# A two-layer macaron block on one core: the first layer norm with tokens as rows, zero fills on three engines, expert weights loaded in another order

## What is computed

```python
x = L0_attn_x                                                   # (2, 1024, 128)
x = x + 0.5 * _L0_ffn_ref(_layernorm(x, axis=-1), L0_ffn_Wg, L0_ffn_W_in, L0_ffn_W_out)
x = x + _L0_attn_ref(_layernorm(x, axis=-1), ...)
...
# _layernorm: (x - mean) / sqrt(var + 1e-5), over the 128 features
# _L0_ffn_ref: logits = xf @ Wg; softmax; top 2 of 8 experts; a token is
# dropped where its place in the expert is past C; gates normalised;
# hid = inp @ W_in; a, g = split(hid); out = (gelu(a) * g) @ W_out; y = sum of gates * out
```

## Time and profile before

| | us |
|---|---|
| median of 3 runs (lowest, highest) | 1421.39 (1421.01, 1423.98) |
| profiled execution, own time | 1424.82 |
| its span | 1423.0 |
| PE busy | 1323.8 (93%) |
| VectorE busy | 1005.4 (71%) |
| ScalarE busy | 871.2 (61%) |
| GpSimd busy | 400.2 (28%) |
| mean granted PE clock | 0.981 |

### The profile page before, as it was taken

The page is one execution under the profiler, slowest core; times in us unless marked ns, Lnnn a source line. Parts: engine busy times, 40 slices in busy tenths (PEclk is TensorE's granted clock), DMA queues, the critical chain, the costliest instruction groups (busy, mean ns, idle before and its releaser), DMA issues.

```text
span 1423.0 us, 27091 instructions
## 1 busy us (share of the span) xinstructions
PE 1323.8 (93%) x10934; PEld 562.0 (39%) x10934; DVE 1005.4 (71%) x1516; ACT 871.2 (61%) x1104; POOL 400.2 (28%) x331
## 2 busy tenths in 40 slices
PE   7999998889879999999999998989998999999997
PEld 5344333333324444333444343433433334433443
DVE  3534777889925347698887868688868697978735
ACT  3334347788784454276566767666768676675672
POOL 5554430110011755452220223022305033202010
PEclk8999999999999999999999999999999999999998
DMA  6633101000001731011111010110010101100100
GB/s 177 118 62 70 25 14 31 16 2 2 2 1 39 196 60 34 1 32 24 35 24 24 1 23 1 24 35 10 15 24 1 23 13 24 31 13 19 24 1 15
DMA packets 30291, 45.80 MB, mean 32 GB/s; under 512 B 5892, under 2 KB 10692, under 8 KB 30116
## 3 DMA queue, kind: packets, MB, share of 16 engines
q1 hardware_dynamic: 30168, 44.08, 14.0%
HBM read 25.39 MB, written 1.18 MB: 19 GB/s over the span
## 4 chain that ended last, share of the span: by engine, by line
PE 72%; DVE 11%; ACT 8%; issue 4%; SPq 3%; DMA 2%; POOL 0%; ACTq 0%; DVEq 0%
PE ps L1264 13%; PE ps L1364 11%; PE ps L1309 7%; ACT PR L1442 6%; PE ps L1230 5%; PE ps L1250 5%; PE ps L1231 5%; PE ps L1232 5%; DVE BM L1530 3%; PE ps L1844 3%; PE ps L1328 2%; PE ps L1242 2%; PE ps L1271 2%; PE ps L1375 2%; PE ps L1324 1%
## 5 line engine op out<-in xcount | busy, mean ns | idle before, releaser
L1442 ACT ACTIVATE PR<-ps 128x1024 f32<-128x1024 f32 x432 | 431.2, 1026 | 207.1 <-PE ps L1271 136.4
L1530 DVE TENSOR_REDUCE BM<-ps 128x2 f32<-128x1024 f32 (+2 forms) x384 | 350.4, 950 | 57.0 <-PE ps L1250 55.9
L1264 PE MATMUL ps<-QS,KS 48*128 48x512 f16 (+7 forms) x2688 | 306.1, 329 | 31.7 <-ACT PR L1442 22.5
L1364 PE MATMUL ps<-PR,VS 128*32 128x512 f32 (+3 forms) x2304 | 231.5, 499 | 2.2 <-ACT PR L1442 1.6
L1264 PEld LDWEIGHTS ps<-QS,KS 48*128 48x128 f16 (+1 forms) x2688 | 108.5, 95 | 203.6 <-ACT PR L1442 88.5
L1250 PE MATMUL ps<-KS,QS 48*128 48x128 f16 (+2 forms) x1728 | 161.7, 273 | 19.2 <-DVE BM L1530 10.8
L1523 DVE TENSOR_REDUCE BM<-ps 128x8 f32<-128x1024 f32 x96 | 116.8, 1220 | 39.3 <-PE ps L1250 38.5
L1250 PEld LDWEIGHTS ps<-KS,QS 48*128 48x128 f16 x1728 | 68.0, 94 | 135.3 <-issue 45.8
L1571 POOL TENSOR_TENSOR OS<-OS,RX 128x512 f32<-128x512 f32 x24 | 30.5, 1270 | 273.9 <-ACT RX L1458 273.9
L1230 PE MATMUL ps<-YA,QS 128*128 128x512 f16 x256 | 99.6, 389 | 0.8 <-DVE RX L1489 0.5
L1231 PE MATMUL ps<-YA,QS 128*128 128x512 f16 x256 | 99.2, 388 | 0.0
(11 more groups left out here) (299 smaller groups left out, 2054.9 us busy)
## 6 DMA issues: line engine op xcount, KB each, us to landing
PR<-gates SPq DMA_DIRECT2D x32, 512.0 KB, 12.5
QS<-KS SPq DMA_DIRECT2D x64, 128.0 KB
QS<-KS SPq DMA_DIRECT2D x64, 64.0 KB
WM<-W_in SPq DMA_DIRECT2D x1, 2048.0 KB, 9.0
QS<-HL SPq DMA_DIRECT2D x48, 32.0 KB
KS<-HL SPq DMA_DIRECT2D x48, 32.0 KB
QS<-CT SPq DMA_DIRECT2D x96, 2.0 KB
KS<-KS SPq DMA_DIRECT2D x8, 128.0 KB, 2.4
```

Source lines behind the costliest of these rows:

```text
L1264: ins = pe.matmul(ps[pair][:, w, off:off + cols], KS[rows, ks, kt * P:(kt + 1) * P], QS[rows, qs, (ph + 1) * TT - cols:(ph + 1) * TT], sta ...
L1364: ins = pe.matmul(dst[32 * j:32 * j + 32, TT - cols:TT], v, PR[:, buf, j, off:off + cols], start=(g == 0), stop=(g == NGRP[ph] - 1))
L1442: act.activation(dst, src, ACT.Exp, scale=0.125 if lat else 1.0).then_inc(sig["exp"], 1)
L1530: ins = dve.tensor_reduce(BM[:, ph, p, :, qt - 4 * ph, part], bnk[:, :, off:off + nk * P], AX.X, ALU.max)
```

## The change

- x comes in four DMAs, one a tile, each with its own semaphore. It stands with a token as a row (`XR`, 16 blocks of 128 tokens).
- VectorE takes mean and variance of each row: per tile four `bn_stats` and four `bn_aggr`, on 128 x 128 each. ScalarE takes ln and exp of 128 x 4 values, VectorE makes the shift (L997), and ScalarE scales and shifts four 128 x 128 blocks a tile into `XS`. PE turns `XS` by 16 more transposes, VectorE copies them to `XN`. The matmuls with the mean matrix and the 512-wide square, ln, exp, subtract and multiply of this norm are gone. x itself is still turned and copied to `XT`.
- `KS` is cleared by VectorE (6 pieces, first of all) and GpSimd (10), `QS` by ScalarE (8, before its first-part tasks).
- `W_in` is issued right behind the folded weights and `Wg0`, then `W_out`, then the rest. Waits are for `W_in` alone where the experts start, for the others at `ed` 0.
- 12 of the 16 heads of `pe_comp` stand between the transposes of tiles 1 to 3. The last four, and `pe_comp_out`, are plan tasks (`cmp` 0 and 1). `eh` u waits for them from u = 4, since the ring's places lie over their inputs.
- The constants of `sp_first_consts` are issued behind the eighth `egb`.

The diff, cut to its core:

```diff
+        if kind in ("rlg", "rrk", "rtp", "cmp"):
             return 0
...
+            x = add("DVE", "eh", ("eh", u), x, ("ed", u - self.NHE) if u >= self.NHE else self.staged(u))
...
+            self.add("ACT", "cm", ("cmc", i), self.add("PE", "cm", ("cmp", i), ("rlg",)))
...
-            sp.dma_start(PRf[:, 0:T].rearrange("p (i d) -> p i d", i=NTT),
-                         a["x"].rearrange("(i p) d -> p i d", p=P)).then_inc(s_x0, 16)
+            for t in range(NT):
+                sp.dma_start(XR[:, t, :, :], a["x"].rearrange("(t i p) d -> t p i d", p=P, t=NT)[t]).then_inc(s_x[t], 16)
...
+            sp.dma_start(w_in, a["W_in"].rearrange("e p f -> p e f")).then_inc(s_wm, 16)
...
         def pe_load(pe):
+            pe.wait_ge(s_const, 1)
             for t in range(NT):
+                pe.wait_ge(s_x[t], 16)
+                for i in range(4):
+                    ins = pe.transpose(bank(t)[:, i * P:(i + 1) * P], XR[:, t, i, :], identf[:, :])
+                ins.then_inc(s_ld, 1)
             for t in range(NT):
+                pe.wait_ge(s_xc, t + 1)
+                if t >= 2:
+                    pe.wait_ge(s_xn, t - 1)
+                for i in range(4):
+                    ins = pe.transpose(bank(5 + t % 2)[:, i * P:(i + 1) * P], XS[:, t, i, :], identf[:, :])
+                ins.then_inc(s_ld, 1)
+                if t == 1:
+                    pe.wait_ge(s_wc, 80)
+                if t >= 1:
+                    pe_comp(pe, range(4 * t - 4, 4 * t))
...
+            for h in range(ZDVE):
+                dve.memset(KS[:, h, :].bitcast(F32), 0.0).then_inc(s_zero, 1)
+            stats(0)
             for t in range(NT):
+                if t + 1 < NT:
+                    stats(t + 1)
+                shift(t)
+                if t >= 1:
+                    normal(t - 1)
+                if t < NT - 1:
+                    plain(t)
+            normal(NT - 1)
+            plain(NT - 1)
...
+                for i in range(4):
+                    ins = act.activation(XS[:, t, i, :], XR[:, t, i, :], ACT.Identity, scale=RSTD[:, t, i:i + 1],
+                                         bias=SHIFT[:, t, i:i + 1])
+                ins.then_inc(s_xc, 1)
+            act.wait_ge(s_const, N_CONST)
+            for h in range(8):
+                act.activation(QS[:, h, :].bitcast(F32).rearrange("p (a c) -> p a c", a=2),
+                               goon[:, :].unsqueeze(1).to_broadcast([P, 2, 256]), ACT.Copy, scale=0.0).then_inc(s_zero, 1)
```

More of the change, by code:

```diff
@@ L321, in weights_ready, with staged @@
     def weights_ready(self, u):
+        return None
+    def staged(self, u):
         return None
@@ L428, in weights_ready, with staged @@
         return ("ewl", min(u // 2, E - 1))
+    def staged(self, u):
+        return ("cmp", 1) if u >= 4 else None
     def prologue(self, b):
@@ L675, in priority @@
         if eng == "PE":
-            if kind in ("un", "sc", "pv", "turn", "proj", "eu", "ed", "rlg", "rrk", "rtp"):
+            if kind in ("un", "sc", "pv", "turn", "proj", "eu", "ed", "rlg", "rrk", "rtp", "cmp"):
                 return super().priority(eng, task, t)
@@ L826, in build_program @@
         gate_d = nc.dram_tensor("gates", (4, E, T), F32, kind="Internal").ap()
-        s_x0 = sem("s_x0")
+        s_x = [sem(f"s_x{t}") for t in range(NT)]
         s_w = sem("s_w")
@@ L946, in pool_const, with pe_comp @@
                 ins = pool.memset(desc[:, e:e + 1], float(E - e))
-            pool.memset(epsc[:, 0:1], EPS)
             ins = pool.memset(epsc[:, 1:2], EPS * EPS)
             ins.then_inc(s_const, 1)
+        def pe_comp(pe, heads):
+            for h in heads:
+                ins = pe.matmul(bank(4)[:, h * 32:(h + 1) * 32], wqn[:, h, :], wkb[:, h, :], start=True, stop=True)
+            return ins
         def pe_load(pe):
             pe.wait_ge(s_const, 1)
-            pe.wait_ge(s_x0, 16)
@@ L1488, in dve_attn @@
                     dve.wait_ge(sig["ed"], c("ed", u - plan.NHE))
+                elif not lat and u >= 4:
+                    dve.wait_ge(sig["cmp"], 2)
                 dve.scalar_tensor_tensor(out=ring_he(lat, u), in0=ps[plan.slot[("eu", u)]][:, 1, :],
@@ L1613, in pe_first @@
                     ins.then_inc(sig["val"], 1)
-                else:
+                elif kind == "cmp":
+                    i, = args
+                    if i == 0:
+                        ins = pe_comp(pe, range(H - 4, H))
+                    for h in range(H if i else 0):
+                        g, j = divmod(h, QUAD)
+                        ins = pe.matmul(bank(5)[32 * j:32 * j + 32, g * P:(g + 1) * P], wkb[:, h, :],
+                                        won[h // 8][:, h % 8, :], start=True, stop=True)
+                    ins.then_inc(sig["cmp"], 1)
+                else:
+                    if task == ("eu", 0):
+                        pe.wait_ge(s_xup, NT)
+                    elif task == ("ed", 0):
+                        pe.wait_ge(s_w, N_WFIRST)
                     pe_attn(pe, False, c, plan, task)
@@ L1619, in act_first @@
             table = First.table
-            act.wait_ge(s_wm, 32)
             for task in plan.order["ACT"]:
                 kind, args = task[0], task[1:]
+                if task == ("ewh", 0):
+                    act.wait_ge(s_wm, 16)
                 want = First.TABLE.get(kind, table)
@@ L2361, in _ @@
             sp_load(sp)
-            sp_first_consts(sp)
             sp_first(sp)
```

115 lines of the change are left out of this document (46 added, 69 removed).

## The result

| | before | after |
|---|---|---|
| median of 20 runs (lowest, highest), us | 1424.03 (1420.33, 1431.77) | 1416.82 (1411.55, 1424.27) |
| span of the profiled execution | 1423.0 | 1417.0 |
| router logits end | 32.68 | 28.17 |
| gates leave for DRAM | 43.82 | 40.69 |
| first down projection (`ed` 0) starts | 54.41 | 49.92 |

The ratio after / before is 0.9949 (95%: 0.9933 to 0.9964). Against 1421.4 us that is a gain of 7.2 us (5.1 to 9.5), where 4.4 were forecast: 1414.2 on the scale on which the forecast was 1417.0. The time came out inside the range and on the forecast's side, 2.8 us past it.

The account below looks back on a forecast made before the run. It took the preface's chain of waits through PE, then a full PE from 60 to 150 us, as the bound. Gates leaving at 39.4 instead of 43.8 gain 4.4 us: 1421.4 - 4.4 = 1417.0 us, range 1411 to 1420.

Parts of the forecast that it names:

- Up to the logits: Part from the start to the end of the router logits, forecast to end at 26.1 us instead of 32.7.
- T: The time the router logits end; forecast 26.1 us instead of 32.7.
- Scaling: ScalarE's four 128-wide scaling operations per tile of the norm, put at 1.0 us.
- VectorE has 1.4 us to spare: In the norm, PE's folding was to end last at 19.4 us, with VectorE having 1.4 us of slack.
- Between the logits and the gates: Folding holds rrk, three eu hold rtp; 2.2 of 6.6 us given back, gates stored at 39.4, gain 4.4.
- stays at 1.2 GHz all through: PE's preface, with nothing wide in it and transposes not counted as busy work, was to run at half clock throughout.
- the clock's return: PE's return to full clock in eu 1 to 3: -2.1 us if full at once, +1.8 if all half.
- the early one as a rival: Full clock only from eu 0: gates leave at 36.5, gain 7.3 us; within the full-clock-earlier rival, chance 0.20.
- Absorbed behind 150 us: Rival: behind 150 us VectorE and ScalarE share the bound, half the gain could go; 1419 to 1420 us, chance 0.15.
- reshuffled neighbours: Unknown from tasks changing places in the plan, put at +-1 us on the total.
- Hidden edits: ScalarE's and GpSimd's fills, earlier weights and later constants were to be covered by other work; earlier load alone gives nothing.
- the rival of a full clock from the start: PE at 2.4 GHz from the first folding: gates leave at 30 to 33.4, gain 10.4 and more; full-clock-earlier chance 0.20.

Follow-up runs that it names:

- norm_order: Changed kernel with scaled tile 0 turned before x's tile 3 and tile 3's statistics taken before the first XN copy; 1417.01 us, 0.9965 of the kernel before.
- fills_pool: Changed kernel with all 24 zero fills on GpSimd, none on VectorE or ScalarE; 1420.51 us, 0.9983 of the kernel before.
- wide_between: Changed kernel with extra unread 512-column matmuls on zeros added to PE's preface and logits; 1410.43 us, 0.9902 of the kernel before.
- plan_alone: Kernel before with only the plan's change: the last four heads and pe_comp_out become tasks behind eu 0; 1422.13 us, 0.9985 of the kernel before.
- before_again: Kernel before, unedited, profiled once more; 1422.12 us, one run.
- gates_first: Changed kernel with VectorE's copy of the turned gates moved directly behind router step 21; 1419.47 us, 0.9971 of the kernel before.
- fold_ahead: Changed kernel with all folding ahead of the logits again and the old plan, new norm and fills kept; 1423.07 us, 1.0003 of the kernel before.
- after_again: Changed kernel, unedited, timed and profiled once more; 1418.22 us, 0.9964 of the kernel before.
- weights_late: Changed kernel with W_in and W_out issued last again; 1418.69 us, 0.9954 of the kernel before.

## Why the prediction was right

**Up to the logits: right in shape, 2.1 us short.** T was forecast at 26.1 and came at 28.17. Fills (0.53 each, 3.19 in all, for 3.8 forecast), statistics (1.2 a tile, for 1.4) and shift (0.13) were no dearer than taken. Two terms were too small. *Scaling:* four ScalarE activations of 128 columns took 1.65 us, not 1.0. I had scaled 0.55 for 512 columns down; 0.41 for 128 says that most of it doesn't go with width. *x:* the last quarter landed at 9.09 (7.4 to 9.1 in the traces where it is on the chain), not 7.7; with the logits 19.1 us behind it, that alone is 1.4 of the 2.1 us. With PE in order, the turn of the scaled tile 0 stood behind it, and so did VectorE, with the statistics of tile 3 and the shift of tile 2 queued. norm_order took that coupling out and had the folding done at 19.37. That the forecast said 19.4 is luck in part, since it priced the scaling 0.65 us a tile too low. I had written "VectorE has 1.4 us to spare"; it had none. The logits took 6.92, for 6.7.

**Between the logits and the gates: right in mechanism.** The folding held `rrk` until 34.38, 6.2 us behind the logits (6.0 forecast). `rtp` had no idle time before it and stood behind `eu` 3, 11.5 us behind the logits (12.2 forecast). 1.4 us of the 4.5 were given back (2.2 of 6.6 forecast). The two errors cancel in part: the gates left at 40.69, where 39.4 was forecast, so 3.1 us sooner than before instead of 4.4, and in the executions where the clock returned early at 37.0 to 38.0. `et` 0 started 7.8 us behind the store (7.9 forecast), PE stood 0.66 us for it (1.1 forecast), and `ed` 0 came 4.5 us earlier though the gates were only 3.1 earlier, because PE wasn't held for `rtp` and its clock didn't fall again. `ed` 4 now stood ahead of `eu` 12, as forecast, and both were done at about 57.6 instead of 61.46, 3.9 earlier (4.4 forecast).

**The clock: right for after ahead of the logits, too narrow behind them.** The preface ran at half clock all through in after, and in five more of the seven profiled executions that have the new norm and nothing added on PE. The seventh is fills_pool: PE had run transposes and nothing else, and its next four took 0.66 us and the folding behind them 1.07, before the clock fell again ahead of the turn at 13.60. "TensorE: Matmul & The Clock Gate", Part 4: PE-mode transpose, of the Trainium skill, says that transposes don't count as busy work for the clock. After agrees with it (0.22 to 0.28 us a transpose, 0.11 to 0.17 in wide_between), fills_pool doesn't, so the prediction's "stays at 1.2 GHz all through" holds in most executions, not in all. It cost nothing there, since PE stood 1.29 us for ScalarE right behind. The folding passes of 32 columns and the logits of 8 ran at half clock from 16.5 to 28.2 us in after. What I had wrong is that I took the clock's return as one value with a tolerance (-2.1 to +1.8). It is two cases, 30 and 37 us, in the same kernel, 2.9 us of lead apart (0.75 of them x), and I had booked the early one as a rival instead of as part of the forecast.

**From 60 to 200 us: right.** The lead of 4.1 holds. **Absorbed behind 150 us: wrong way round.** I put reshuffled neighbours at +-1 us, and gave 0.15 to half of the gain being lost. They gave 3.3 us net by 441 in the trace of after, and 2.2 in plan_alone. That is the term of the sum that was mis-sized most, and with it fails the sign that every landmark between 100 and 400 us would be earlier by the same amount. It is of the size of the 2.8 us between 1417.0 and 1414.2, though these are themselves within what a second timing of the same kernel moved. I had seen the swaps in the plan, but judged them by the amount of work ahead of each task, which says nothing on who waits for whom: 19 waits for ScalarE instead of 17 can't be read from it.

**Hidden edits: right.** Earlier weights gave nothing. ScalarE's fills ran from 17.63 to 21.88 and GpSimd's from 16.10 to 20.78, beside folding and logits that lasted to 28.17, as forecast.

**The sums.** Three don't come out as written. Gates that leave at 30 to 33.4 give a gain of 10.4 to 13.8, so 1407.6 to 1411.0 for the rival of a full clock from the start, not 1410.4. The clock's return "if full at once" was put at -2.1 us, but VectorE asks for the turned gates only at 36.8, so by the prediction's own rows it is worth 1.5. And the listed unknowns add up to 1413.4 to 1420.7, wider than the 1414.5 to 1419 drawn from them. None of this touches the 1417.0.

That the total fell where it did is luck in part: up to the gates the change gave 3.1 us and not 4.4, and the plan's order, taken as nothing give or take 1, added 3.3.

The gain has three parts, and only the first was forecast: what the preface and the gates give up to 200 us, 4.1 or 7.0 by the clock and x's landing; what the plan's order gives on the way to 441, 3.3 in after and 2.2 in plan_alone; and the unchanged rest, which moves it by some 3 us either way in a single execution. What stays open is what decides, from one execution to the next, whether the clock returns at 30 or at 37 us, and whether x's last quarter lands at 7.4 or at 9.1.

## What to carry to other kernels

Where work is queued behind a late transfer on an in-order engine, follow who waits for *that* engine as well: here a quarter of x on PE held VectorE, and through it ScalarE. When a change moves tasks in a planned order, compare the lists of waits of the bound engine, stretch by stretch, of a kernel that has the new order alone: neither the tasks' counts nor a single total tells it. And look at the same kernel's trace twice before giving a microsecond to a cause, and at what else differs between two traces beside the edit (x's landing moved by 1.7 us between two of them here); of the two halves of this change each alone gave nothing clear of the noise, and only experiments with one half each could show that.

## What the runs showed of the hardware

- The granted clock, as the profile gives it, reads full in stretches that the durations show to be at half. In after, with matmuls 0.43 us apart:

```profile
36.00:37.00 1.00, 1.00 (x4) 0.38 (x3) 0.93 (x3) 0.00 (x0) 0.00 (x0) 1.00 0.00 0
```

  In the earlier trace rows the same stretch of before read 0.58. In doubt, go by the spacing of equal matmuls.
- Among the executions without extra work on PE, the spacing of expert matmuls fell from 0.43 to 0.22 us at 36.6 to 37.6 us in six (before, before_again, after, gates_first, norm_order, fold_ahead), though these matmuls began anywhere between 26.3 and 33.2 us. In three (after_again, weights_late, fills_pool) PE was at full clock already in the folding behind `eu` 0, at 29 to 31 us. In plan_alone, where 3.7 us of narrow folding come 2.6 us after the first wide matmuls (at 32.69), they were still 0.43 us apart at 44.19.
- A `bn_stats` of 128 x 128 took 0.21 us in a row of four, a `bn_aggr` 0.09, an activation of 128 x 128 with scale and bias per partition 0.41, one of 512 columns 0.53 to 0.55.
- In fills_pool PE reached full clock by 10.64 us with nothing but transposes run until then (four of them took 0.66 us there, 1.12 at 13.60); in six other executions of the new norm without extra work on PE the same four took 1.06 us or more.
- Four loads of 256 KB issued first, one after the other, landed in the same order of issue at 3.7 to 3.9, 4.5 to 4.8, 5.8 to 6.9 and 7.4 to 9.1 us: the last varied by 1.7 us from one execution to the next.
